# Cross attention with image-prompt tokens: V products as loop tasks, U products five slots later

## What is computed

```python
q = heads(hidden_states @ W_q)
k_t, v_t = heads(text_ehs @ W_k), heads(text_ehs @ W_v)
probs_t = softmax(einsum('bhsd,bhtd->bhst', q, k_t) * attn_scale)
text_out = einsum('bhst,bhtd->bhsd', probs_t, v_t)
k_ip, v_ip = heads(ip_ehs @ W_k_ip), heads(ip_ehs @ W_v_ip)
attn_scores = einsum('bhsd,bhnd->bhsn', q, k_ip) * attn_scale
qsem = l2norm(einsum('bhst,bte->bhse', probs_t, text_ehs))
sem = einsum('bhse,bne->bhsn', qsem, l2norm(ip_ehs))
probs_ip = softmax(attn_scores + 0.5 * sem) * spatial_mask
out = (text_out + einsum('bhsn,bhnd->bhsd', probs_ip, v_ip)) @ W_out + b_out + hidden_states
```

## Time and profile before

| what | us |
|---|---|
| median of three runs | 313.21 |
| lowest and highest | 312.33, 313.55 |
| the profiled execution's own time | 312.51 |
| its span in the trace | 310.7 |
| PE busy in the span | 300.6 (97%) |
| ACT busy | 273.1 (88%) |
| DVE busy | 270.9 (87%) |
| POOL busy | 211.7 (68%) |

### The profile page before, as it was taken

How to read it: one execution, slowest core, us unless ns; L and a number is a source line. 1 busy time by engine, 2 the same in 40 slices (tenths; PEclk the granted TensorE clock), 3 DMA queues, 4 the chain that set the end, 5 groups by cost and what they waited for, 6 DMA issues and landing times.

```text
span 310.7 us, 8849 instructions
## 1 busy us (share of the span) xinstructions
PE 300.6 (97%) x2306; PEld 291.4 (94%) x2306; DVE 270.9 (87%) x1867; ACT 273.1 (88%) x1160; POOL 211.7 (68%) x373
## 2 busy tenths in 40 slices
PE   7899999999999999999999999999999999998976
PEld 6897989989999999999999999999999999998964
DVE  7848878888898989998898889888989899998895
ACT  3647789999999999999999999999999999999941
POOL 3055457688977797879787896879777977675200
PEclk9999999999999999999999999999999999999999
DMA  6992000000010212021202020110102120010011
GB/s 216 338 287 55 4 1 13 1 3 21 20 58 25 63 36 63 24 66 32 66 22 66 31 57 34 30 58 26 51 24 63 36 65 23 24 32 22 23 43 65
DMA packets 15129, 17.01 MB, mean 55 GB/s; under 512 B 2592, under 2 KB 14536, under 8 KB 15080
## 3 DMA queue, kind: packets, MB, share of 16 engines
q1 hardware_dynamic: 15040, 16.38, 17.8%
q10 hardware_dynamic: 40, 0.07, 0.1%
HBM read 10.55 MB, written 5.24 MB: 51 GB/s over the span
## 4 chain that ended last, share of the span: by engine, by line
PE 87%; DVE 4%; ACT 4%; DMA 2%; POOL 1%; issue 1%; SPq 1%; POOLq 0%
PE gv_ps L1093 25%; PE mi_ps L1128 13%; PE mi_ps L1052 12%; PE sc_ps L1072 11%; PE et_ps L1080 10%; PE mi_ps L1106 3%; PE mi_ps L1030 2%; ACT e_sb L627 2%; DMA x_nat<-in_x 2%; PE gv_ps L1210 2%; DVE place_ctxT L796 1%; PE gv_ps L1177 1%; PE sc_ps L1189 1%; PE mi_ps L1032 1%; PE mi_ps L1236 1%; PE et_ps L1210 1%
## 5 line engine op out<-in xcount | busy, mean ns | idle before, releaser
L627 ACT ACTIVATE e_sb<-sc_ps,negmax 128x60 f32<-128x60 f32 x640 | 152.3, 352 | 5.0 <-DVE negmax L788 3.7
L796 DVE CUSTOM_DVE_ANT_0 place_ctxT<-gv_ps,e_sb 128x60 f32<-128x60 f32 x640 | 100.9, 214 | 16.9 <-PE gv_ps L1093 15.3
L1093 PE MATMUL gv_ps<-tab,place_w 128*128 128x160 f32 x640 | 113.3, 299 | 0.1
L1093 PEld LDWEIGHTS gv_ps<-tab,place_w 128*128 128x128 f32 x640 | 94.0, 189 | 1.6 <-ACT place_w L645 0.7
L1072 PE MATMUL sc_ps<-km,qs 128*128 128x256 f32 x320 | 76.8, 321 | 0.0
L645 ACT COPY place_w<-et_ps 128x256 f32<-128x256 f32 x160 | 68.4, 428 | 0.3
L788 DVE TENSOR_REDUCE negmax<-sc_ps 128x4 f32<-128x240 f32 x160 | 63.6, 397 | 0.0
L1080 PE MATMUL et_ps<-ident,e_sb 128*128 128x128 f32 x320 | 61.7, 274 | 1.7 <-ACT e_sb L627 1.3
L796 DVE DVE_READ_ACCUMULATOR2_ANT quad<- 128x1 f32 x640 | 53.0, 83 | 0.0
L636 ACT COPY fin<-gv_ps 128x80 f32<-128x80 f32 x160 | 43.7, 273 | 7.1 <-DVE quad L796 5.9
L1072 PEld LDWEIGHTS sc_ps<-km,qs 128*128 128x128 f32 x320 | 48.2, 191 | 0.2 <-issue 0.2
(11 more groups left out here) (180 smaller groups left out, 557.5 us busy)
## 6 DMA issues: line engine op xcount, KB each, us to landing
x_nat<-in_x SPq DMA_DIRECT2D x16, 320.0 KB, 3.2
out<-place_w SPq DMA_DIRECT2D x32, 160.0 KB, 1.8
place_ctx<-in_ctx SPq DMA_DIRECT2D x4, 256.0 KB, 3.9
place_w<-in_L_xattn_W_v SPq DMA_DIRECT2D x1, 640.0 KB, 7.7
place_w<-in_L_xattn_W_k SPq DMA_DIRECT2D x1, 640.0 KB, 9.6
place_w<-in_L_xattn_W_k_ip SPq DMA_DIRECT2D x1, 640.0 KB, 9.5
place_w<-in_L_xattn_W_v_ip SPq DMA_DIRECT2D x1, 640.0 KB, 11.1
place_ctxT<-in_L_xattn_W_out SPq DMA_DIRECT2D x1, 640.0 KB
```

Source lines behind the costliest of these rows:

```text
L627: last = nc.scalar.activation(e_sb[:, slot, TOK * j:TOK * j + T], sc_ps[:, bank, TOK * j:TOK * j + T], ACT.Exp, bias=negmax[:, slot, j:j + 1])
L796: last = v.tensor_tensor_reduce(out=junk[:, u % 2, j, 0:T], in0=gv_ps[:, u % 2, TABW * j:TABW * j + T], in1=e_sb[:, u % ERING, TOK * j:TOK ...
L1093: last = mm(gv_ps[:, u % 2, 2 * TABW * r:2 * TABW * r + 2 * TABW], eT[:, u % TRING, P * r:P * r + P], tab[:, b % 2, h:h + 2, :].rearrange( ...
```

## The change

The V products leave the prologue and become three tasks, `("vip", m, 0)`, in slots 1, 2 and 4. Each has a bank of `mi_ps`, waits for its release like the other tasks, and is spread by DVE on its own, at the end of slot 2, 3 and 5. They no longer wait for `k_lo`. The U products stand in slots 6, 9, 11, 12 and 14; the first waits for all three spreads. `place_u(0)` still waits for three copied U products and so comes in DVE's slot 12. The split of batch 0 moves to slot 18 of ACT and slot 19 of DVE. No instruction is added or taken away; two waits are added and the three spreads signal one by one.

```diff
-        U_AT, U_PARTS = (1, 2, 4, 6, 9), (0, 2, 4, 1, 3)
+        for m, at in enumerate((1, 2, 4)):
+            MISC[at] = ("vip", m, 0)
+        U_AT, U_PARTS = (6, 9, 11, 12, 14), (0, 2, 4, 1, 3)
...
+                    "vip": (vip_made, n + 1), "u": (u_copied, n + 1),
...
-            return b if s == (12 if b else 14) and b < B else None
+            return b if s == (12 if b else 18) and b < B else None
...
-                if u == 0:
-                    spread_vip()
...
+                if kind == "vip":
+                    spread_vip(m)
                 if kind == "u":
                     copy_u(m)
...
-                    pe.wait_ge(k_lo, 4)
+                pe.wait_ge(*bank_released(("vip", m, 0)))
+                bank = mi_ps[:, misc_bank(("vip", m, 0)), 0:B * NIP]
...
             scores(2)
-            vip_product(0)
             x_transposes(1, 0)
             x_transposes(1, 1)
             pe.wait_ge(k_lo, 2 * GROUPS)
             e_transposes(1)
             scores(3)
-            vip_product(1)
-            vip_product(2)
...
+                if kind == "vip":
+                    vip_product(n)
```

More of the change, by code:

```diff
@@ L320, in bank_released @@
             return {"x": (xT_lo, 2 * index + n + 1), "q": q_copied_at(n, index) if by_pool else q_lo_at(n, index), "v": (v_copied, PAIRS),
-                    "u": (u_copied, n + 1),
+                    "vip": (vip_made, n + 1), "u": (u_copied, n + 1),
                     "at": (attnT_lo, index + 1), "o": (y_made, index + 1)}[kind]
@@ L855, in k_low, with spread_vip @@
                                                op0=ALU.mult, op1=ALU.subtract).then_inc(k_lo, 1)
[L857 to L868, removed]
+            def spread_vip(m):
+                dve.wait_ge(pre_vip, m + 1)
+                hp, rows = QROWS[m] // D, QROWS[m]
+                vip = mi_ps[0:rows, misc_bank(("vip", m, 0)), 0:B * NIP].rearrange("p (b n) -> p b n", n=NIP)
+                v.tensor_copy(vip_bd[0:rows, m, 0:B].unsqueeze(2), vip[:, :, NDIF:NIP])
+                v.tensor_tensor(
+                    vip_bd[0:rows, m, B:B + B * hp * NDIF].rearrange("p (b h n) -> p b h n", h=hp, n=NDIF),
+                    vip[:, :, 0:NDIF].unsqueeze(2).to_broadcast([rows, B, hp, NDIF]),
+                    head_of_row[0:rows, 0:hp].unsqueeze(1).unsqueeze(3).to_broadcast([rows, B, hp, NDIF]),
+                    ALU.mult).then_inc(vip_made, 1)
             def copy_u(n):
@@ L1219, in vip_product @@
                     pe.wait_ge(in_wvip, DMA)
-                    pe.wait_ge(k_lo, 4)
+                pe.wait_ge(*bank_released(("vip", m, 0)))
+                bank = mi_ps[:, misc_bank(("vip", m, 0)), 0:B * NIP]
                 for c in range(EC):
-                    last = mm(BANKS[5][0:QROWS[m], 32 * m:32 * m + 32].rearrange("p (b n) -> p b n", n=NIP),
+                    last = mm(bank[0:QROWS[m]].rearrange("p (b n) -> p b n", n=NIP),
                               wvip[:, c, P * m:P * m + QROWS[m]], ip_dif[:, c], start=c == 0, stop=c == EC - 1)
-                if m == QC - 1:
-                    last.then_inc(pre_vip, 1)
+                last.then_inc(pre_vip, 1)
             def u_product(n):
```

## The result

| | median us | lowest, highest | executions |
|---|---|---|---|
| before | 313.08 | 312.08, 313.55 | 22 |
| changed | 314.56 | 313.02, 315.64 | 22 |

The forecast was +0.6 us, or 313.8; the time, 314.56, lies in the range, in its upper half.

A forecast was written before the change was run, and what follows sets the result against it. PE bounds to slot 10 and after 72 us, DVE and ACT between; -0.23 + 0.54 - 0.33 + 0.44 + 0.2 + 0.2 - 0.2 gives +0.6 us, 313.8 against a 313.21 median. Range 312.5 to 315.2 us.

The forecast's parts named there:

- PE's sum comes out whole: Rival for the whole kernel: PE's waits move along, the 1.97 us of added work stay, 315.2 to 315.6 us; chance 0.12.
- POOL's wait: Slot 20: the scores' 0.22 us wait for POOL's split of q goes, with its restart, about -0.2 us.
- Prologue, -0.23: Before slot 0: without the V products the second x transposes start earlier, limited by a bank DVE leaves; 0.23 us gained.
- Slots 1, 2 and 4, +0.27, +0.27 and -0.33: Full PE slots: V products replace U products, costing 0.27 us twice, then gaining 0.33 as the 64-row product leaves.
- PE comes to slot 11 at -0.02: Start of slot 11: prologue and slots 1, 2 and 4 together leave PE 0.02 us earlier than before.
- Slot 11 starts within 0.1 us of where it does now: Sign to look for in the changed kernel: PE's slot 11 start moves by no more than 0.1 us.
- DVE's copy behind the normalization, ACT's entry +0.44: DVE slot 12: the third U product's copy, 0.40 us plus some 0.04, delays ACT's exponentials of unit 16 by 0.44.
- the forecast's own third step: ACT slot 14 loses the split, but late table products and maxima of unit 18 keep the shift at about +0.6 us.
- Split of 0.36 us in slot 18: ACT slot 18 takes on the 0.36 us split; with 0.15 us of slack, it adds +0.2 us.
- The transfers cost nothing: SP issues batch 0's six transfers from 60.0 to near 64.9 us; ACT wants them about 69, so no cost.
- The 64-row product takes its 0.37 us along to slot 11: Slots 4 and 11: the extra 0.37 us belongs to the 64-row U product and moves with it.
- The clock: Rival: PE's idling before the x transposes and slot 0 lowers its clock, costing +1.5 us or more; chance 0.03.

The follow-up runs named there:

- e5: Changed kernel, plus 16 identity transposes in PE's pause at the end and the 64-row U product's operands zero-padded to 128 rows: 313.24 us.
- e8: Changed kernel, plus 16 identity transposes in PE's end pause and, in slots 1, 2 and 4, the V product behind the table products: 313.35 us.
- e6: Changed kernel, plus 16 identity transposes in PE's end pause and the split of batch 0 in ACT's slot 19 instead of 18: 313.16 us.
- e4: Kernel before, plus 16 identity transposes in PE's end pause, U products in slots 6, 9, 11, 12, 14 and split in slot 18; V products unmoved: 311.78 us.
- e3: Kernel before, with the transposes of unit 32 issued four times over in slot 30 to delay PE ahead of the end pause: 313.55 us.

## Why the prediction was right, and where its sum fell short

The mechanism was right in the main, and the size was half of what was measured: +1.24 us in the loop where the sum said +0.6. That the time lies in the range all the same is owed to the range's width, which took in part of the rival in which PE's sum comes out whole, and not to the sum. From the mark, the 0.61 us between the forecast of +0.62 and the +1.23 of the table are: 0.08 in the prologue, 0.37 behind the V products, 0.04 in slots 11 to 19, 0.16 for the split and -0.05 for POOL's wait (0.01 is rounding).

- **Prologue, -0.23: measured -0.15.** The x transposes wait for the bank that DVE leaves, at 34.29 + 0.44 = 34.73 us, as said. I took 0.05 us from there to PE's start; the chain of work shows 0.14 (34.73 to 34.87).
- **Slots 1, 2 and 4, +0.27, +0.27 and -0.33: measured +0.36, +0.36 and -0.14.** This is the step that failed, and it carries 0.37 of the missing 0.61 us. I took the V product's 0.81 and 0.58 from the prologue, where what stood behind them was short, and left the table products behind them at 0.54. They take 0.63, 0.62 and 0.74. The row for it lay before me in the earlier trace rows: table products of 0.74 behind a small product. I put that down to 64 rows. e5 shows that this is true of the U product, and e8 and the rows of the weight loads that a V product has such a successor too.
- **PE comes to slot 11 at -0.02: measured +0.44.** Those two steps and nothing else. "Slot 11 starts within 0.1 us of where it does now" was a sign that did not come.
- **DVE's copy behind the normalization, ACT's entry +0.44.** The exponentials of unit 16 start at 60.13 us, 26.42 from the mark against 25.45: +0.97. That is 0.44, the 0.46 that PE brings along, and 0.07. But this is not where the chain enters ACT. ACT stands still before units 16 and 18, both times for DVE's maxima, and the chain follows PE through slot 13 and comes to ACT only with unit 18. It takes the path of the forecast's own third step: the table products behind the q product, forecast done at 62.1 us, are done at 62.10, and the maxima of unit 18, forecast for 63.4, at 63.41. The mark itself is 0.48 us earlier here, so both are late by nearly 0.5 us, the 0.46 that PE brings along. That the net of slots 11 to 19 came out within 0.04 us, +0.68 for +0.64, is this step's merit; the 0.44 of DVE's copy is no term of it. ACT's idle time in the changed kernel:

```profile
60.13 0.91 ACT L629 ACTIVATE e_sb<-sc_ps,negmax 128x60 f32<-128x60 f32 x4 [0.43 <-DVE negmax L790]
...
63.44 0.92 ACT L629 ACTIVATE e_sb<-sc_ps,negmax 128x60 f32<-128x60 f32 x4 [0.28 <-DVE negmax L790]
```

- **Split of 0.36 us in slot 18: measured +0.36**, in slot 20 of the table, and e6 takes just that back. I had given it 0.15 of slack; there was none. Slot 20 starts at 71.56 us when its 37.37 are counted from the mark of the kernel before, just inside the 71.6 from which I would have been wrong. **POOL's wait, -0.2: measured -0.25.**
- **The transfers cost nothing**, as said: SP issues them from 59.73 us on, and the split starts at 68.98 directly behind ACT's copy of transposes.
- **The 64-row product takes its 0.37 us along to slot 11**: confirmed by the chain of work and by e5.
- **The rival "PE's sum comes out whole"** came closer than the 0.12 I gave it. Against e4, which has the same U slots, the V products' 1.70 us come out whole; against the kernel before, 0.46 us of it are won back, as in e4, since the later U products fill waits.
- **The clock.** I looked for it in the prologue, where it stays at 1.00 with PE busy for 2.06 of 3.90 us. Against it I cited the pause at the end, by one profile in which it had not fallen. In about half of the executions of that same kernel the mean clock is 0.995 (16 of 29, 14 of 29 and 6 of 11).

Of the 1.5 us between the medians, 1.24 are the loop. The rest fits the clock at the end, which fell in more executions of the changed kernel and cost more in them (1.15 us between its two medians; 0.52, 0.78 and 0.87 between those of the kernel before in the three groups). That it falls more often is not shown beyond chance, and why it costs more is open.

## What to carry to other kernels

Price a product that moves together with what comes behind it: eight small products with weights of their own, or one with 64 rows, left the loads of their successor late, by 0.09 and 0.20 us here. Taking 2.20 us of V products out of the prologue, where most of it stood in waits, gave back 0.15 us, and in full slots they took their whole length and 0.37 more; the half of this change that went the other way, from full slots into waits, was worth 0.5 us by itself (e4). Where an engine stops for some two us, one profile did not tell what its clock does afterwards; the mean clock of many executions did.

## What the runs showed of the hardware

- In two profiles (the changed kernel and e3) TensorE's granted clock fell to the lower level behind a pause of 2.17 or 2.18 us; in the profile of the kernel before it stayed at 1.00 behind the same pause. By the mean clock, 0.995 against 1.00, it fell in 36 of 69 executions of the kernel before; with PE later by 0.57 us ahead of the pause, in 6 of 12. With sixteen transposes of the identity in the pause the mean clock stayed at 0.998 or more in 80 of 83 executions of nine kernels; the other three took 1.9 to 2.0 us more than the rest of their kernel.
- A product whose contraction has 64 rows and the product behind it take 0.71 + 0.74 us, with zeros up to 128 rows 0.54 + 0.54. In e5 the zeros cost nothing that the rows show.
- Eight products with 128 columns of weights each and 32 moving columns take 0.81 us and the table products behind them 0.08 to 0.09 more; with 64 columns of weights 0.58 and 0.20 more.
- Weight loads start 0.43 us ahead of the table products where these take 0.54 us, 0.19 ahead where they take 0.63, and 0.07 to 0.08 ahead where they take 0.74.
